# Combining a token's two expert rows in a mixture-of-experts kernel: picks ordered by expert number, the reload of the rows in two parts, VectorE alone

## The reference

```python
logits = xt @ router_w + router_b
scores = softmax(logits, axis=-1) + router_bias
g = scores.reshape(T, 4, 4)
_, gidx = top_k(g.max(axis=-1), 2)                 # two of four groups
masked = where(keep[:, :, None], g, -inf).reshape(T, 16)
_, idx = top_k(masked, 2)                          # two experts per token
vals = take_along_axis(scores, idx, axis=1)
gate = zeros((T, 16)).at[arange(T)[:, None], idx].add(vals)
for each expert e:
    h = silu(xt @ w1[e] + b1[e]) * (xt @ w2[e] + b2[e])
    y = y + gate[:, e:e+1] * (h @ w3[e] + b3[e])
z = silu(xt @ sw1 + sb1) * (xt @ sw2 + sb2) @ sw3 + sb3
return x + y + z
```

## Time and profile before

| | us |
|---|---|
| median of 3 runs | 169.54 |
| lowest, highest | 169.12, 170.14 |
| the profiled execution | 169.93 |
| its span, first to last instruction | 168.2 |
| time of it outside the span | 1.73 |

### The profile page before, as it was taken

How to read it: one execution, slowest core, us unless ns; L and a number is a source line. 1 busy time by engine, 2 the same in 40 slices (tenths; PEclk the granted TensorE clock), 3 DMA queues, 4 the chain that set the end, 5 groups by cost and what they waited for, 6 DMA issues and landing times.

```text
span 168.2 us, 2537 instructions
## 1 busy us (share of the span) xinstructions
PE 147.6 (88%) x742; PEld 114.9 (68%) x743; DVE 97.6 (58%) x231; ACT 58.7 (35%) x117; POOL 57.6 (34%) x71
## 2 busy tenths in 40 slices
PE   3899899999979999999989999999999977999100
PEld 3678688888767778887867857866777753888000
DVE  2663675558957578978128854334534533436994
ACT  4532422714622151154543423433343321026600
POOL 6810140000000020435205765665476572209700
PEclk9999999999999999999999999999999999999955
DMA  4999938999863599998301557877674452389964
GB/s 173 302 370 380 394 76 321 394 420 414 314 230 146 146 389 365 406 432 276 111 5 66 184 191 248 212 267 250 217 242 169 149 169 81 125 305 392 363 257 179
DMA packets 16507, 42.59 MB, mean 253 GB/s; under 512 B 2192, under 2 KB 2192, under 8 KB 16240
## 3 DMA queue, kind: packets, MB, share of 16 engines
q1 hardware_dynamic: 11392, 25.41, 41.5%
q0 software_dynamic: 3616, 12.06, 22.0%
q10 hardware_dynamic: 1488, 4.98, 7.5%
HBM read 33.53 MB, written 8.91 MB: 252 GB/s over the span
## 4 chain that ended last, share of the span: by engine, by line
PE 62%; DMA 13%; DVE 8%; issue 8%; POOL 4%; ACT 2%; SPq 0%; POOLq 0%; DVEq 0%
PE bank L909 29%; PE bank L1076 14%; DMA xg_sb<-xt_rows,slot_tok 6%; PE bank L1091 6%; PE bank L1066 4%; DMA condW_raw<-in_condWT 3%; PE bank L965 2%; DVE x_sb L882 2%; DMA yg_sb<-y_rows 2%; POOL yg_sb L449 2%; POOL y_rows L421 2%; PE bank L955 2%; DMA y_rows<-y_sb,slot_row 2%; PE bank L976 1%; DVE x_sb L876 1%
## 5 line engine op out<-in xcount | busy, mean ns | idle before, releaser
L1076 PE MATMUL bank<-w_sb,xgT_sb 128*128 x144 | 37.4, 383 | 1.8 <-issue 1.8
L1076 PEld LDWEIGHTS bank<-w_sb,xgT_sb 128*128 128x128 f32 x144 | 25.4, 190 | 13.2 <-issue 10.6
L421 POOL DMA_INDIRECT y_rows<-y_sb,slot_row x18 | 18.6, 1031 | 24.9 <-DVE y_sb L828 24.9
L415 POOL DMA_INDIRECT xg_sb<-xt_rows,slot_tok x20 | 19.4, 968 | 11.9 <-issue 8.0
L816 DVE TENSOR_TENSOR pre_sb<-bank,b_sb 128x256 f32<-128x256 f32 x18 | 7.6, 425 | 25.4 <-PE bank L1076 25.2
L1091 PE MATMUL bank<-w_sb,hT_sb 128*128 x36 | 18.5, 596 | 0.5 <-ACT hT_sb L567 0.5
L909 PE MATMUL bank<-condW_h,xT_h 128*128 128x512 f32 x32 | 13.4, 418 | 1.1 <-DVE condW_l L638 0.9
L828 DVE COPY y_sb<-bank 128x512 f32<-128x512 f32 x18 | 12.3, 684 | 1.5 <-PE bank L1091 1.5
L398 POOL MEMSET gate<- 128x768 f32 x1 | 0.7, 741 | 36.2 <-PE bank L976 36.2
L909 PE MATMUL bank<-xtT_h,sw_h 128*128 128x512 f32 x32 | 13.0, 407 | 0.0
L559 ACT COPY xgT_sb<-bank 128x512 f32<-128x512 f32 x18 | 10.5, 586 | 6.8 <-PE bank L1066 3.9
(11 more groups left out here) (164 smaller groups left out, 285.9 us busy)
## 6 DMA issues: line engine op xcount, KB each, us to landing
w_sb<-in_w SPq DMA_DIRECT2D x8, 1024.0 KB, 9.1
w_sb<-in_w ACTq DMA_DIRECT2D x2, 2048.0 KB, 14.5
yg_sb<-y_rows SPq DMA_DIRECT2D x8, 512.0 KB, 6.5
xt_rows<-xt_ring SPq DMA_DIRECT2D x8, 256.0 KB, 4.3
b_sb<-in_b SPq DMA_DIRECT2D x1, 2048.0 KB, 10.8
x_sb<-in_x SPq DMA_DIRECT2D x8, 256.0 KB, 2.9
out<-x_sb SPq DMA_DIRECT2D x8, 256.0 KB, 2.1
xT_raw<-in_xT SPq DMA_DIRECT2D x3, 512.0 KB, 5.0
```

What stands on the lines that cost most here:

```text
L415: pool.indirect_dma_start(xg_sb[:, b % 4, :], None, xt_rows, bass.IndirectOffsetOnAxis(ap=slot_tok[:, b:b + 1], axis=0)).then_inc(gathered ...
L421: pool.indirect_dma_start(y_rows, bass.IndirectOffsetOnAxis(ap=slot_row[:, b:b + 1], axis=0), y_sb[:, b % 2, :], None).then_inc(y_scattere ...
L1076: mm = pe.matmul(bank[2 + s % 2][:, 0:2 * INTER], xgT_sb[:, s % 2, k, :], w12_sb[:, bass.ds(e * W12 + k * 2 * INTER, 2 * INTER)], start=(k ...
```

## The change

- `choose` makes `pick`, the smaller and the larger of the two expert numbers (two new DVE instructions per pair of tiles, four pairs), and `sel` is built from it. Pick 0 of a token is now its lower expert, pick 1 its higher one. `val` holds their scores.
- After the fourth block DVE computes from `base` of expert E - 1, in six instructions on single numbers, two semaphore values, and signals `low_known`.
- SP waits for `y_scattered` to reach those two values and then reloads the rows of pick 0 in four transfers of 512 KB (two tiles each); then it waits as before and reloads the rows of pick 1 in eight transfers of 256 KB.
- ACT and POOL have no part in the end any more. DVE does, per tile, `add_shared`, `add_low` and `add_high`, the latter two as `scalar_tensor_tensor`, and each but the last waits for the one before it on the same tile.
- The shared expert's output uses all eight banks, so PE's wait for DVE from the fifth tile on is gone.
- The tiles are stored in order 0 to 7.

```diff
@@ the sync engine
-            sp.wait_ge(slot_row_ready, 1)
+            by_tile = y_rows[0:K * T, :].rearrange("(k i p) d -> k p i d", k=K, p=P)
+            sp.wait_ge(low_known, 1)
+            low_e = sp.value_load(eid[0:1, LOW_EVEN_AT:LOW_EVEN_AT + 1], min_val=16 * LOW_BLOCKS // 2, max_val=16 * (BLOCKS + 1) // 2)
+            low_o = sp.value_load(eid[0:1, LOW_ODD_AT:LOW_ODD_AT + 1], min_val=16 * LOW_BLOCKS // 2, max_val=16 * BLOCKS // 2)
+            sp.wait_ge(y_scattered[0], low_e)
+            sp.sem_inc(low_stored, 1)
+            sp.wait_ge(y_scattered[1], low_o)
+            sp.sem_inc(low_stored, 1)
+            sp.wait_ge(low_stored, 2)
+            for n in range(TILES // 2):
+                sp.dma_start(yg_sb[:, 2 * n:2 * n + 2, 0, :], by_tile[0][:, 2 * n:2 * n + 2]).then_inc(low_in[n], 16)
...
             for i in range(TILES):
-                sp.dma_start(yg_sb[:, i], y_rows[0:K * T, :].rearrange("(k i p) d -> i p k d", k=K, p=P)[i]
-                             ).then_inc(y_in[i], 16)
+                sp.dma_start(yg_sb[:, i, 1, :], by_tile[1][:, i]).then_inc(high_in[i], 16)
@@ choose
+                for k, order in enumerate((ALU.min, ALU.max)):
+                    then(dve.tensor_tensor(pick[:, tiles, k], best_at[:, tiles, 0], best_at[:, tiles, 1], order))
@@ the vector engine, before hidden(1)
-            then(dve.tensor_tensor(tmp[:], sel[:, 0], over_experts(best[:, :, 0]), ALU.mult))
-            then(dve.tensor_tensor(sc1[:], sel[:, 1], over_experts(best[:, :, 1]), ALU.mult))
-            then(dve.tensor_tensor(sc[:], tmp[:], sc1[:], ALU.add))
+            then(dve.tensor_tensor(sel_sc, sel[:], sc[:].unsqueeze(1).to_broadcast([P, K, TILES, E]), ALU.mult))
+            then(dve.tensor_reduce(val[:], sel_sc, AX.X, ALU.add))
+            then(dve.tensor_tensor(sc[:], sel_sc[:, 0], sel_sc[:, 1], ALU.add))
@@ the first four blocks, at the end of each turn
+                if b == UNROLL - 1:
+                    then(dve.tensor_scalar(low_blocks[:], base[0:1, E - 1:E], 1.0 / P, None, ALU.mult))
+                    then(dve.tensor_scalar(low_even[:], low_blocks[:], -2, None, ALU.bitwise_and))
+                    then(dve.tensor_copy(low16[:], low_even[:]))
+                    then(dve.tensor_scalar(low16[:], low16[:], 8.0, None, ALU.mult))
+                    then(dve.tensor_copy(eid[0:1, LOW_ODD_AT:LOW_ODD_AT + 1], low16[:]))
+                    dve.scalar_tensor_tensor(out=eid[0:1, LOW_EVEN_AT:LOW_EVEN_AT + 1], in0=base[0:1, E - 1:E],
+                                             scalar=16.0 / P, in1=low16[:], op0=ALU.mult, op1=ALU.subtract
+                                             ).then_inc(low_known, 1)
@@ the end on the vector engine
+            add_shared(0)
+            for i in range(TILES - 2):
+                add_shared(i + 1)
+                add_low(i)
+            add_high(0)
+            add_high(1)
+            add_shared(TILES - 1)
+            add_low(TILES - 2)
+            add_low(TILES - 1)
+            for i in range(2, TILES):
+                add_high(i)
```

More of the change, by code:

```diff
@@ L164, in program @@
         best_at = sb("best_at", [P, TILES, TOP], U32)
+        pick = sb("pick", [P, TILES, K], U32)
+        val = sb("val", [P, K, TILES])
         tmp = sb("tmp", [P, TILES, E])
@@ L232, in program @@
         y_scattered = [sem(f"y_scattered{s}") for s in range(2)]
-        shared_done, acc_shared, y_in = sem("shared_done"), sem("acc_shared"), [sem(f"y_in{i}") for i in range(TILES)]
+        shared_done, acc_shared = sem("shared_done"), sem("acc_shared")
+        low_in = [sem(f"low_in{i}") for i in range(TILES // 2)]
+        high_in = [sem(f"high_in{i}") for i in range(TILES)]
         acc_done, out_stored = sem("acc_done"), sem("out_stored")
@@ L245, in shared_bank @@
         def shared_bank(i):
-            return bank[(7, 0, 1, 2)[i % 4]]
+            return bank[(7, 0, 1, 2, 3, 4, 5, 6)[i]]
         def last_group(eng):
@@ L446, in _ @@
                             scatter(g * UNROLL + n)
-            for n, i in enumerate(POOLED):
-                pool.wait_ge(scaled, K * (n + 1))
-                pool.tensor_tensor(yg_sb[:, i, 0, :], yg_sb[:, i, 0, :], yg_sb[:, i, 1, :], ALU.add).then_inc(pair_added, 1)
         @block.scalar
@@ L598, in _ @@
             drained(act, drain)
-            for i in POOLED:
-                act.wait_ge(y_in[i], 16)
-                for k in range(K):
-                    act.activation(yg_sb[:, i, k, :], yg_sb[:, i, k, :], ACT.Copy, scale=best[:, i, k:k + 1]
-                                   ).then_inc(scaled, 1)
         @block.vector
@@ L693, in choose @@
                 dve.wait_ge(dve_step, made[0])
+                for k, order in enumerate((ALU.min, ALU.max)):
+                    then(dve.tensor_tensor(pick[:, tiles, k], best_at[:, tiles, 0], best_at[:, tiles, 1], order))
                 by_pick = [P, K, 2, E]
-                then(dve.tensor_tensor(sel[:, :, tiles], best_at[:, tiles, 0:K].rearrange("p i k -> p k i").unsqueeze(3).to_broadcast(by_pick),
+                then(dve.tensor_tensor(sel[:, :, tiles], pick[:, tiles].rearrange("p i k -> p k i").unsqueeze(3).to_broadcast(by_pick),
                                        cols_i[:, 0:E].unsqueeze(1).unsqueeze(1).to_broadcast(by_pick), ALU.is_equal))
@@ L871, in add_shared, with add_low, add_high @@
                 dve.tensor_tensor(x_sb[:, i, :], x_sb[:, i, :], shared_bank(i)[:], ALU.add).then_inc(acc_shared, 1)
-            def add_pooled(i):
-                dve.wait_ge(pair_added, POOLED.index(i) + 1)
                 dve.wait_ge(acc_shared, i + 1)
-                dve.tensor_tensor(x_sb[:, i, :], x_sb[:, i, :], yg_sb[:, i, 0, :], ALU.add).then_inc(acc_done, 1)
-            def add_experts(i):
-                dve.wait_ge(y_in[i], 16)
-                dve.wait_ge(acc_shared, i + 1)
-                for k in range(K):
-                    ins = dve.scalar_tensor_tensor(out=x_sb[:, i, :], in0=yg_sb[:, i, k, :],
-                                                   scalar=best[:, i, k:k + 1], in1=x_sb[:, i, :],
-                                                   op0=ALU.mult, op1=ALU.add)
-                    if k < K - 1:
-                        then(ins)
-                ins.then_inc(acc_done, 1)
-            for i in range(5):
-                add_shared(i)
-            add_pooled(0)
-            add_shared(5)
-            add_pooled(1)
-            add_shared(6)
-            add_experts(3)
-            add_shared(7)
-            add_pooled(2)
-            add_pooled(4)
-            add_pooled(5)
-            add_experts(6)
-            add_experts(7)
+            def add_low(i):
+                dve.wait_ge(low_in[i // 2], 16)
+                then(dve.scalar_tensor_tensor(out=x_sb[:, i, :], in0=yg_sb[:, i, 0, :], scalar=val[:, 0, i:i + 1],
+                                              in1=x_sb[:, i, :], op0=ALU.mult, op1=ALU.add))
+            def add_high(i):
+                dve.wait_ge(high_in[i], 16)
+                dve.scalar_tensor_tensor(out=x_sb[:, i, :], in0=yg_sb[:, i, 1, :], scalar=val[:, 1, i:i + 1],
+                                         in1=x_sb[:, i, :], op0=ALU.mult, op1=ALU.add).then_inc(acc_done, 1)
+            add_shared(0)
[9 more added lines that the diff above has]
+                add_high(i)
         @block.tensor
```

20 lines of the change are left out of this document (11 added, 9 removed).

## The result

The changed kernel takes **173.44 us** (median of 4 runs, 172.48 to 175.64) where the kernel before takes 169.57 in the runs beside it. The ratio is **1.0204, 95% interval 1.0162 to 1.0246**: slower by 2.0%. (The run of 175.64 us was in a slower state of the chip and does not count for the ratio.) The forecast was 170.8 with a range up to 171.9. The direction was right, the size was not: +3.5 us by the ratio, 3.9 by the two medians, where 1.25 was forecast. The profiled execution took 173.53 us, its span 171.8.

What follows compares the result with a forecast made beforehand. The prediction took the reload and DVE's combining to set the end, with PE busy in the block loop. End 0.35, loop's head 0.85 and routing 0.05 gave +1.25 us on 169.54: 170.8 us, range 169.2 to 171.9.

Steps and rivals of the forecast that it cites:

- Part 1: Start of the reload: expert 15's `base` is the end of all 18 blocks, so the low half starts no earlier; gain nothing.
- The rival's price of it: Rival that the early reload does work, low rows there when DVE starts combining: -2.0 at the end, 168.4 us; chance 0.06.
- Part 2: The end: DVE alone runs 22 instructions behind the first low transfer, without a gap; +0.35 us, bounds -1.1 to +1.05.
- the end moves from 165.75 to 166.1: +0.35: DVE's last instruction at the combining: old end from the trace, new end from priced instructions; +0.35 us.
- I take 150.15 for it: First low reload transfer, again 512 KB after the same wait, taken as usable at 150.15 us as before.
- at most 0.1 of queue: Last stores: six come 0.68 us apart, 256 KB take 0.69, each lands in 2.0 to 2.1; at most 0.1 us builds up.
- Part 3: Loop's head: six small instructions delay the sequencer's register loads, first bias 1.1 us later, PE stands 0.85 us; +0.85.
- the upper bound of 1.1: Loop's head: the cost is 1.1 us instead of 0.85 if PE's pipeline must refill as well.
- The rival "the head hides them": Loop's head hides the six instructions, by loading ahead or regaining the stall; only the end counts, 169.9 us; chance 0.26.
- Part 4: Routing: the added `choose` instructions and new `val` block fit into existing waits; 0 up to 0.1 us, taken as 0.05.
- the last one, waits or a DMA that come worse than the rows say: Rival: DVE's waits at the end, or a worse-timed DMA, cost 1 us more, 171.9 us; chance 0.08.
- rule on the slow form: Rival at the end: 16 `scalar_tensor_tensor` on two SBUF inputs take twice 0.74 us, 11.8 us later, some 182.6; chance 0.01.

Runs made afterwards that it cites:

- e2: Changed kernel with `base` of expert 14, the last in use on these inputs, in place of expert 15; 173.70 us, ratio 1.0189.
- e3: Changed kernel with `base` of expert 14 and the six small instructions moved ahead, before the first blocks; 172.05 us, ratio 1.0109.
- e7: e3 with the low rows in eight transfers of 256 KB, each behind a later block's copy, instead of four of 512 KB; 169.02 us, ratio 0.9939.
- again_after: The changed kernel run once more, unedited; median 172.75 us, span 171.1.
- e1: Changed kernel without the six small instructions, low rows waiting for the same final values as the high ones; 171.58 us, ratio 1.0138.
- again_before: The kernel before run once more, unedited; span 167.8 us, median 169.99.
- after: The changed kernel's first, profiled run, unedited; median 173.44 us, profiled execution 173.53.
- e10: Changed kernel with the six small instructions moved ahead, to where DVE waits for PE before the first blocks; 172.03 us, ratio 1.0132.
- e9: Changed kernel with the stores of the odd tiles started by ACT; 172.37 us, ratio 1.0155.
- e6: Kernel before with only the six small instructions added at the loop's head; 170.98 us, ratio 1.0045.
- e4: Kernel before with only the ordered picks and the new `val`; 169.41 us, ratio 0.9971.
- e8: e7 with an order of DVE's 24 end instructions that starts on low rows and waits only on the same tile; 164.64 us, ratio 0.9663.

## Why the prediction missed, point by point

**Part 1 was right.** The low reload started at 148.82, 2.81 us after the last scatter's issue, at the same distance from the last copy as in the kernel before (3.78 us in both). The early reload gave nothing. The rival's price of it was wrong, though. With `base` of expert 14 it is not 168.4 but 173.70 (e2), since the rival let 2 MB run beside the gathers for free. A transfer that is moved into another stage has to be priced against the transfers that it meets there, and e3 and e7 show that the burst makes most of it.

**Part 2, the sum over the 22 instructions was right to 0.1, and both its starting point and the old end that it was set against were wrong.** Counted: 16.0 us from the first low row to DVE's end. Measured: 168.61 - 152.58 = 16.03, and the same in again_after and e1. The step that failed is "the end moves from 165.75 to 166.1: +0.35". It sets a sum for the new end against one execution of the old one. The old end varies, and which of DVE's instructions are stretched beside POOL differs: the first two `scalar_tensor_tensor` take 3.39 us in this trace and 2.20 in that of again_before. From last copy to DVE's end it takes 22.90 in this trace, but 22.36, 21.82 and 22.74 in the three others with the old end, a mean of 22.46 (22.63 of the two unedited ones). The new end takes 23.55 to 23.74 in five traces, a mean of 23.61, where the forecast had 166.1 - 142.85 = 23.25. The difference is +1.15 (+0.97 of the unedited ones), not +0.35, and the two faults have about equal shares in it. That of the new end is mostly the first landing, "I take 150.15 for it": issue to first use is 3.7 to 3.9 us with the new rows and 3.4 to 3.5 with the old ones, +0.3. Both sets are transfers of 512 KB; why the new ones are later wasn't tried.

**The stores, "at most 0.1 of queue", are the step that failed by most.** DVE's end to the span's end grew from 2.4 to 2.5 us (four traces) to 3.1 to 3.2 in after, again_after and e10, and by 0.1 only in e1 and e9. That is +0.7 in both traces of the changed kernel, and its cause stays open. The earlier trace rows has 2.0 and 2.1 as the least and the median of the landings of stores that were mostly further apart, and 6.8 as the greatest, which the forecast left out; one row for six close ones wasn't there, and the bound should have been wider.

**Part 3: the mechanism was right, the size too small.** The first bias came 1.93 us behind the start of the sixth instruction (102.95 - 101.02), where 101.5 - 99.9 = 1.6 had been reckoned. Most of that is in the register loads: the one of the expert number took 546 ns, not the 311 it takes in the kernel before, while the one of `top` took 311, not 378. So PE waited 0.95, not 0.85, and its turn comes 1.11 us late by the distance. That this meets the upper bound of 1.1 is luck: the bound stood for a refilled pipeline of PE, and the rows show a late bias. e6 shows the same alone (+1.08), e1 and e10 show it gone. The size varies, and in the five traces with the six at the head it goes with the load of the expert number: 332 ns and a distance of 3.88 in e2, 374 and 4.10 in e9, 468 and 4.22 in e6, 518 and 4.20 in again_after, 546 and 4.25 in after. What makes that load longer wasn't tried. The rival "the head hides them" is out.

**Part 4 was right**: e4 shows no cost. The first gather's wait of 1.56 us did not recur, so it counts as chance, but it stood in the profiled execution. Of the rivals the last one, waits or a DMA that come worse than the rows say, was the nearest to what came: the first landing and the last stores were worse in both traces of the changed kernel. It had been priced at 1 us.

**The sum again**, by means of the two traces of each kernel, 171.45 - 168.0 = 3.45 us:

```
term                                   forecast   measured
to the first turn of gathered rows     0.05       +0.75 (79.80 - 79.05; 1.12 and 0.37 apart)
loop's head                            0.85       +1.09
rest of the blocks                     0          -0.08
last copy to DVE's end                 0.35       +0.97
DVE's end to the end of the span       0          +0.72
```

The first row is mostly the one late gather; with 0.37 for both the rows give 3.1 us, and the medians say 2.8 (172.75 - 169.99) to 3.9 (173.44 - 169.57). Where only the head is taken out (e1, e10) the medians stay 1.85 and 2.04 us above the kernel before (0.3 of e1's outside the span): the end with its stores is the larger half of the loss, and I had it as the smaller. The range was too narrow at the top for the same reason: it bounded each price by rows of one trace, but not the spread of the old end itself, and it allowed 1 us for everything unforeseen.

The Trainium skill's rule on the slow form (Vector Engine (DVE) Microarchitecture Reference, section 7: two non-bf16 SBUF sources halve the throughput) does not show in the changed kernel: 752 ns for a `scalar_tensor_tensor` on two SBUF operands beside 0.69 us for a `tensor_tensor`. The Trainium skill's rule on SBUF interfaces that POOL shares with VectorE (GPSIMD Engine Reference, section 1) fits: with POOL silent, no DVE instruction at the end was stretched.

## What to carry to other kernels

Small instructions that wait for one another are cheap on the engine and dear in front of its sequencer's register loads; put them where the engine waits for data anyway. A reload that is moved beside a stage with gathers must be spread over it: 2 MB at once cost 4 us in two profiled executions, the same 2 MB in eight pieces about 1 us. It gains only what the instructions behind it no longer wait: with DVE's order as in the changed kernel the time is 0.9 us below the kernel before (e7), with an order that starts on the early rows 5.2 us (e8). And a sum for a new stage is to be set against several executions of the old one if that stage has several engines in contention.

## What the runs showed of the chip beyond that

- A wait of PE of 2.15 us (2.16 in e2) was followed by some 4 us at a granted clock of 0.56 to 0.59 (e3; 0.53 to 0.61 in e2), which nearly doubled its cost. Waits of 0.95 and 1.56 us left the clock at 1.00.
- A gather issued 0.75 us before a burst of four 512 KB transfers on SP's queue took 6.9 us to land, twice as long as the 3.2 to 3.4 of its like.
- A scatter issued at 137.99, beside the last two of the spaced 256 KB transfers, held up the copy behind it until 144.08 (e7), 6.1 us; in the kernel before the scatters land in 2.7 to 2.9.
- The register load of the expert number on DVE's sequencer took 311 ns in the kernel before and 332 to 546 ns behind the six small instructions.
- Stores of 256 KB at 0.68 us from one to the next land 2.0 to 2.1 us after issue in e1, and the last of them after 2.6 (after, again_after, e10, e3) and 2.9 (e2) in others with the same distance between stores.
